# A two-layer transformer kernel on one core: idle products in the stops of layer 0, a tighter routing table, later last weights, and a tail with shared products first

## What is computed

```python
xn = _layernorm(x, axis=-1)
s = _L0_attn_ref(xn, w_qkv, w_out, ln_scale, ln_bias)   # 16 heads of 16, a = (q.k)**4, causal, a / sum(a)
g = _silu(_L0_ffn_ref(xn, ...))                         # 256 -> 2048 -> 256, 4-bit weights with scales
x = x + s * g
xn = _layernorm(x, axis=-1)
s = _L1_attn_ref(xn, Wq, Wk, Wv, Wo, bo)    # 16 heads of 128 in 4 groups, ALiBi, 30*tanh(s/30), causal softmax
g = _silu(_L1_ffn_ref(xn, ...))             # 32 experts, top 4 by sqrt(softplus(logits)) + bias, plus a shared one
x = x + s * g
```

## Time and profile before

| | |
|---|---|
| Time, median of 3 runs | 853.99 us (852.8 to 854.36) |
| The profiled execution: its own time | 852.75 us |
| The profiled execution: span of its trace | 850.9 us |
| Mean granted clock of PE | 0.98 |
| PE busy | 783.5 us (92%) |
| DVE busy | 609.0 us (72%) |
| ACT busy | 465.7 us (55%) |
| POOL busy | 422.4 us (50%) |

### The profile page before, as it was taken

One profiled execution on the slowest core, in us unless ns is written; L12 is line 12 of the kernel. 1 busy time (PEld: TensorE's weight loads), 2 busy tenths in 40 slices (PEclk: granted clock), 3 DMA queues, 4 the chain that ended last, 5 costly groups with the idle time before them and its releaser, 6 DMA issues.

```text
span 850.9 us, 13950 instructions
## 1 busy us (share of the span) xinstructions
PE 783.5 (92%) x4871; PEld 637.8 (75%) x4871; DVE 609.0 (72%) x1077; ACT 465.7 (55%) x822; POOL 422.4 (50%) x479
## 2 busy tenths in 40 slices
PE   7999999978788878899998999999999997989996
PEld 6776776754233257698998989989999997978884
DVE  7588868457999867878788877997777543445455
ACT  4433342278888733686855565556665724555431
POOL 1767827333555445456444534576656514555530
PEclk9999999997999899999999999999999999999999
DMA  5211194000000040000000000010101599444107
GB/s 183 75 38 37 38 304 126 1 1 1 1 1 2 1 127 27 25 7 25 7 19 7 27 7 7 26 44 32 39 32 46 210 244 382 132 124 112 46 11 237
DMA packets 50115, 59.81 MB, mean 70 GB/s; under 512 B 13559, under 2 KB 41084, under 8 KB 50048
## 3 DMA queue, kind: packets, MB, share of 16 engines
q1 hardware_dynamic: 45488, 50.49, 19.2%
q0 software_dynamic: 4560, 8.44, 2.8%
HBM read 41.11 MB, written 21.86 MB: 74 GB/s over the span
## 4 chain that ended last, share of the span: by engine, by line
PE 58%; DVE 8%; POOL 6%; ACT 6%; issue 4%; DMA 3%; POOLq 0%; ACTq 0%; DVEq 0%; SPq 0%
PE ps L786 12%; PE ps L516 9%; PE ps L518 8%; PE ps L517 8%; PE ps L879 4%; PE ps L876 3%; PE ps L910 3%; POOL A L1777 2%; DMA xa<-xg_scratch 2%; PE ps L613 2%; PE ps L698 2%; PE ps L558 2%; PE ps L858 1%; DVE cap L1477 1%; PE ps L795 1%
## 5 line engine op out<-in xcount | busy, mean ns | idle before, releaser
L786 PE MATMUL ps<-V,P 128*128 128x129 f32 x1152 | 150.7, 276 | 0.0
L1131 ACT ACTIVATE cap<-cap 128x1024 f32<-128x1024 f32 (+7 forms) x128 | 87.1, 680 | 110.3 <-DVE cap L1477 106.6
L786 PEld LDWEIGHTS ps<-V,P 128*128 128x128 f32 x1152 | 143.3, 192 | 2.7
L1477 DVE SCALAR_TENSOR_TENSOR cap<-dist,ps 128x1024 f32<-128x1024 f32 (+7 forms) x128 | 95.3, 750 | 28.7 <-PE ps L518 20.8
L1701 POOL TENSOR_SCALAR_AFFINE_SELECT P<-P 128x128 f32<-128x128 f32 x128 | 38.3, 299 | 143.7 <-ACT P L1136 143.3
L1833 POOL DMA_INDIRECT y_scratch<-y_sb,aux_s x63 | 62.1, 985 | 70.8 <-ACT y_sb L1176 40.3
L1136 ACT ACTIVATE P<-cap 128x1024 f32<-128x1024 f32 (+7 forms) x128 | 87.6, 685 | 4.1
L516 PE MATMUL ps<-q_hi,k_hi 128*128 128x512 f32 x192 | 71.8, 374 | 6.4 <-DVE cap L1477 5.0
L518 PE MATMUL ps<-q_lo,k_hi 128*128 128x512 f32 x192 | 67.0, 349 | 0.0
L517 PE MATMUL ps<-q_hi,k_lo 128*128 128x512 f32 x192 | 66.7, 347 | 0.0
L1629 DVE TENSOR_SCALAR gu<-ps 128x256 f32<-128x256 f32 (+1 forms) x63 | 28.9, 458 | 47.6 <-PE ps L876 16.8
(11 more groups left out here) (288 smaller groups left out, 2104.7 us busy)
## 6 DMA issues: line engine op xcount, KB each, us to landing
xg_scratch<-blank SPq DMA_DIRECT2D x1, 8127.0 KB, 31.1
xa<-xg_scratch SPq DMA_DIRECT2D x63, 128.0 KB
ew<-in_experts SPq DMA_DIRECT2D x3, 1920.0 KB, 12.3
y<-y_scratch SPq DMA_DIRECT2D x8, 512.0 KB, 5.8
pk<-in_packed SPq DMA_DIRECT2D x8, 384.0 KB, 3.1
pks<-in_scales SPq DMA_DIRECT2D x8, 384.0 KB, 4.1
ew<-in_experts SPq DMA_DIRECT2D x1, 3072.0 KB, 17.5
wqk<-in_wqk SPq DMA_DIRECT2D x20, 128.0 KB, 2.0
```

The source lines that it names most:

```text
L786: last = pe.matmul(ps[:, 4 + r % 2, o:o + D1 + 1], P1[:, h % 2, a:a + P], V1[:, j, h // REP, :], start=(j == 0), stop=(j == t))
L1131: act.activation(cap[:, n % 2, 0:w], cap[:, n % 2, 0:w], ACT.Tanh, scale=1.0 / (CAP * float(D1) ** 0.5))\
L1477: dve.scalar_tensor_tensor(out=cap[:, n % 2, 0:w], in0=dist[:, 0:w], scalar=slope, in1=psf[:, 1024 * (n % 2):1024 * (n % 2) + w], op0=ALU. ...
```

## The change

The change has five parts.

- **Early copies.** The copies of q and k of tiles 0 and 1 into `stack` move from behind the network of layer 0 into its steps 27 and 29 (ACT) and one step later (DVE). `turn_stack(0)` now stands ahead of PE's wait for `fT_ready`.
- **Idle products.** `keep_clock` gets new calls in layer 0's attention: one ahead of the scores of units 3 to 6, two ahead of each quad's turn (behind the wait for the banks, ahead of the wait for `o_raw`), two ahead of the last `turn_o`, one ahead of the projection. `add_nothing` adds products of the zero tile `blank` to bank 7 before the outputs of rows 4 and 5 of each quad.
- **Routing.** The two operations that follow the copy of the logits become a part of their own (number 37) at step 7. The four parts of the top 8 stand in one step each. Most later parts, the ranks and the sends stand about 8 steps earlier.
- **Last weights.** SP asks for the last group of experts behind the rows of block 15, where it was behind those of block 11.
- **Tail.** The loads of `y4` no longer wait for each other. The eight shared products stand ahead of all sums, each in a bank of its own, and `sum_rows` adds only the pairs. The pairs have four buffers. DVE multiplies by s one tile later, and POOL adds to x.

```diff
             for b in range(NT, NBLK):
                 sp.wait_ge(xg_ps, b - NT + 1)
                 load_rows(b)
-                if b == NT + 3:
+                if b == NT + 7:
                     load_experts(5)
...
             for t in range(NT):
-                if t >= YLOADS:
-                    sp.wait_ge(pair_ready, t - YLOADS + 1)
-                sp.dma_start(y4[:, t], y_dram.rearrange("(k t p) d -> t p k d", k=TOPK, p=P)[t]).then_inc(in_y4[t % YLOADS], 16)
+                sp.dma_start(y4[:, t], y_dram.rearrange("(k t p) d -> t p k d", k=TOPK, p=P)[t]).then_inc(in_xg[t], 16)
...
+            def add_nothing(n):
+
+                for _ in range(n):
+                    pe.matmul(ps[:, 7, 0:D], ident[:], blank[:, 0:D], start=False, stop=False)
...
+                if 3 <= n < 3 + LAG:
+                    pe.wait_ge(g0_ready, NT)
+                    keep_clock(1, 7)
                 bank_pair(("scores", n))
...
+                if half == 1 and j in (4, 5):
+                    add_nothing(2 if j == 4 or g == H0 // QUAD - 1 else 1)
                 pe.wait_ge(s0_four, BY_DVE0[DONE0[R] - 1])
...
             def turn_out0(g):
 
+                b = bank_pair(("turn", g))
+                keep_clock(2, b)
                 pe.wait_ge(o0_copied, g + 1)
-                b = bank_pair(("turn", g))
...
-            pe.wait_ge(fT_ready, 2 * NC)
             for t in range(NT):
                 turn_stack(t)
+                if t == 0:
+                    pe.wait_ge(fT_ready, 2 * NC)
                 turn_f0(t)
...
+            def shared_down(t):
+                if t == 0:
+                    pe.wait_ge(hT_copied, NBLK - NE)
+                    pe.wait_ge(y_copied, NBLK)
+                if t == 6:
+                    pe.wait_ge(s_added, NT * H1 // PAIR)
+                pe.matmul(sum_at(t), hs[:, t, 1, :], expert(NE)[:, 2, :], start=True, stop=False)
+
             def sum_rows(t):
                 pe.wait_ge(pair_ready, t + 1)
-                if t == 0:
-                    pe.wait_ge(y_copied, NBLK)
-                if t >= 2:
-                    pe.wait_ge(fth_ready, t - 1)
-                o = ps[:, 6 + t % 2, 0:D]
                 for i in range(2):
-                    pe.matmul(o, ident[:], yp[:, t % 2, i, :], start=(i == 0), stop=False)
-                pe.matmul(o, hs[:, t, 1, :], expert(NE)[:, 2, :], start=False, stop=True).then_inc(fin_ps, 1)
+                    last = pe.matmul(sum_at(t), ident[:], pairs_of(t)[:, i, :], start=False, stop=(i == 1))
+                last.then_inc(fin_ps, 1)
...
+                if s in STACK_STEPS:
+                    stack_hi(STACK_STEPS.index(s))
...
-                link(dve.tensor_copy(lg[:], o.rearrange("p (t e) -> p t e", t=NT)))
-                link(dve.tensor_scalar(r_a[:], lg[:], -1.0, None, ALU.mult))
-                dve.tensor_tensor(r_a[:], r_a[:], lg[:], ALU.max).then_inc(lg_read, 1)
+                dve.tensor_copy(lg[:], o.rearrange("p (t e) -> p t e", t=NT)).then_inc(lg_read, 1)
...
+                if s - 1 in STACK_STEPS:
+                    stack_lo(STACK_STEPS.index(s - 1))
...
-                dve.tensor_tensor(yp[:, t % 2], y4[:, t, 0:2], y4[:, t, 2:4], ALU.add).then_inc(pair_ready, 1)
...
+                if t >= 4:
+                    dve.wait_ge(fin_ps, t - 3)
+                dve.tensor_tensor(pairs_of(t), y4[:, t, 0:2], y4[:, t, 2:4], ALU.add).then_inc(pair_ready, 1)
...
+            for t in range(NT):
+                pool.wait_ge(mixed, NT + t + 1)
+                pool.tensor_tensor(x_tok[:, t, :], x_tok[:, t, :], mix1_b[:, t % 2, :], ALU.add).then_inc(x_ready, 1)
...
+STACK_STEPS = (2 * U0 - 5, 2 * U0 - 3)
+SUM_BANKS = (2, 3, 4, 5, 6, 7, 0, 1)
...
+          + [36, 37, 38, 39, 44, 44, 45, 46, 47]
...
-RANKS_AT = 7
+RANKS_AT = 6
```

More of the change, by code:

```diff
@@ L112 @@
 YRING = 6
-YLOADS = 4
 NO_ROW = 1 << 20
@@ L281, in build_program, with pairs_of @@
         y_sb = sb("y_sb", [P, YRING, D])
+        def pairs_of(t):
+            return yp[:, t % 2] if t % 4 < 2 else gu[:, t % 2].rearrange("p k m n -> p (k m n)").rearrange("p (i d) -> p i d", i=2)
         yp = sb("yp", [P, 2, 2, D])
@@ L367, in build_program @@
         in_aux = sem("in_aux")
-        in_y4 = [sem(f"in_y4{i}") for i in range(YLOADS)]
         y_sent = [sem(f"y_sent{i}") for i in range(YRING)]
@@ L567, in turn_f0, with keep_clock @@
                 last.then_inc(f_ps, 1)
+            def keep_clock(n, bank):
+                for _ in range(n):
+                    pe.matmul(ps[:, bank, 0:D], x_tok[:, 0, 0:P], x_tok[:, 0, :], start=True, stop=True)
+            def add_nothing(n):
+                for _ in range(n):
+                    pe.matmul(ps[:, 7, 0:D], ident[:], blank[:, 0:D], start=False, stop=False)
             def score_spans(n):
@@ L658, in gate_up @@
                 last.then_inc(done, 1)
-            def keep_clock(n, bank):
-                for _ in range(n):
-                    pe.matmul(ps[:, bank, 0:D], x_tok[:, 0, 0:P], x_tok[:, 0, :], start=True, stop=True)
             pe.wait_ge(in_x[0], 16)
@@ L971, in collect_f, with stack_hi @@
                     act.activation(fT[:, c, 0:HALF], ps[:, 4 + 2 * c, :], ACT.Copy).then_inc(fT_ready, 1)
+            def stack_hi(t):
+                act.wait_ge(qk_ready, t + 1)
+                if t >= 2:
+                    act.wait_ge(stk_ps, 4 * (t - 1))
+                for m, places in ((0, slice(0, 4, 2)), (1, slice(0, 2))):
+                    src = qk_tok[:, t, m * D:(m + 1) * D].rearrange("p (h a d) -> p h a d", h=H0, a=1)
+                    act.activation(stack[:, t % 2, m, :, places, :].bitcast(F32R),
+                                   src.to_broadcast((P, H0, 2, D0)), ACT.Copy).then_inc(stk_hi, 1)
             def high0(J):
@@ L1029, in _ @@
                     act.activation(hsd[:], hv[:], ACT.Sqrt).then_inc(sd_ready, 1)
+                if s in STACK_STEPS:
+                    stack_hi(STACK_STEPS.index(s))
             collect_f(2 * U0, dn0_ps, f0T)
             for t in range(NT + 1):
-                if t < NT:
-                    act.wait_ge(qk_ready, t + 1)
-                    if t >= 2:
-                        act.wait_ge(stk_ps, 4 * (t - 1))
-                    for m, places in ((0, slice(0, 4, 2)), (1, slice(0, 2))):
-                        src = qk_tok[:, t, m * D:(m + 1) * D].rearrange("p (h a d) -> p h a d", h=H0, a=1)
-                        act.activation(stack[:, t % 2, m, :, places, :].bitcast(F32R),
-                                       src.to_broadcast((P, H0, 2, D0)), ACT.Copy).then_inc(stk_hi, 1)
+                if 2 <= t < NT:
+                    stack_hi(t)
                 if t >= 1:
```

61 lines of the change are left out of this document (36 added, 25 removed).

## The result

The changed kernel takes 846.84 us (median of 6 runs, 846.22 to 847.45) where the kernel before took 852.67 us in the same comparison (median of 6 runs, 849.89 to 854.36). The ratio is 0.9926, with a 95% interval from 0.9905 to 0.9948. It is faster, by 5.8 us, and not by the 14.15 us of the prediction. 846.84 lies outside the range of 833.5 to 844.5. One execution of the experiments (of `last_quad_products_only`) took 1951.24 us and counts in no ratio.

The account below looks back on a forecast made before the run. PE was taken as the bound, busy 92% of the span, so gains come only from its idle or low-clock time. Gains 2.2 + 1.6 + 1.7 + 7.15 + 1.5 = 14.15 gave 838.6 to 839.8, middle 839.2 us, range 833.5 to 844.5.

Parts of the forecast that it names:

- Early copies, -2.2: Before layer 0's first scores: ACT sheds four copies, so 2.19 of PE's 2.58 us wait goes.
- Idle products, -3.0 + 1.4: Layer 0's attention: full clock gives back 3.0 us, products ahead of the turns cost 1.4, net gain 1.6.
- the cost of 1.4: Two idle products ahead of each turn cost 0.48 us in each of layer 0's inner three quads.
- The page's rule of half: Rival: PE sets the pace at low clock, so half the low time returns, 8.5 us instead of 3.0; 833.7 us, 7%.
- Routing, -1.7: Layer 1's attention: respaced routing parts shorten two PE waits that end with DVE, by 1.2 and 0.5 us.
- spread over four steps I take 1.2 of it: Layer 1: the top 8's four parts, one a step, take 1.2 us off PE's wait of 1.69 us.
- The last rival: Slower than before: newly placed routing makes PE wait at each part, 0.42 us each, 15.5 us in all; 856.4 us, 3%.
- Last weights, -7.15: Among the experts: asking for the last weights later removes the stall at block 12 and its low clock, 7.15 us.
- Tail, -1.5: End of the program: the rebuilt tail gains 1.5 us, taken between bounds of 0.2 and 3.7.
- With the 2.16 the end is 847.2: Tail without DVE and POOL holding each other: 2.16 us follow the last addition, end 847.2, a gain of 3.7.
- the serial tail: Rival: in the tail no DVE and POOL work overlaps, 1.85 us a tile, end about 850.7, gain 0.2; 840.5 us, 14%.
- all but the last two: The list of chances without its last entries, slower routing (3%) and something unseen (3%); the range was given 90%.

Follow-up runs that it names:

- last_quad_products_only: The changed kernel with layer 0's new idle products kept only at the end of the last quad; 850.91 us, ratio 0.9984.
- the first experiment: The changed kernel, but DVE adds to x again in the tail and POOL has nothing left to do there; 840.27 us, ratio 0.9855.

## Why the prediction was wrong, step by step

- **Early copies, -2.2:** right, 2.81 measured, 2.82 when undone. The whole wait of 2.58 us went, since PE's turn no longer waits for the copies of the sums either. Its row shows no wait at all.
- **Idle products, -3.0 + 1.4:** the direction was right, the size was not: 4.04 in the two spans, 5.0 when undone. The mis-sized term is the cost of 1.4. The two products at each turn do delay the first turn by 1 us, and a quad at full clock is not longer for it (23.33 against 23.32). The prediction says of the low clock that ACT sets the pace there; that the same slack takes in the products was not tested apart. Besides, the windows left out the end of the last quad, from 288.64 to 300.24, where the clock was 0.85. That quad alone gave 2.83 us where 1.22 was taken. The page's rule of half (the Trainium skill, "TensorE: Matmul & The Clock Gate", section "Terms") would have been worth 10.3 us here: the low time in the windows of the kernel before is 10.2 + 3.5 + 7.0 = 20.7 us. A fifth of that came back in the two spans, so the rule is far off in this stage. Whether it holds where PE sets the pace, no run here shows.
- **Routing, -1.7:** the wrong sign, +2.7. The step that failed is "spread over four steps I take 1.2 of it". The old wait did go, but the prediction looked only at what stood in front of the waits it knew, and not at what the new table puts in front of the next ones: the reciprocal of 1.75 us and two more parts of two operations each, in steps 30 and 31, ahead of the sums of the first output projection. With these three parts moved away 0.9 us came back. The other term, 0.5 for the wait of 1.98 us, came out. The last rival named the mechanism and priced it at every part, which was far too much. It needed a price at two or three places.
- **Last weights, -7.15:** the size came out (6.84), and the stall is gone from the place that was named, but the size is luck in good part. With both edits undone and the rest of the change kept, 4.9 of the 6.84 us stayed, and no run shows what gives them. The mechanism was half right too. By the prediction the moved load alone brings block 16 in time by 0.3 us (722.5 against 722.8). Alone it left a wait of 1.1 to 1.5 us there in four kernels. The tighter routing, with its earlier load of `aux_s`, takes the whole stall away by itself.
- **Tail, -1.5:** the wrong sign, +5.16, and the larger error. The step that failed is "With the 2.16 the end is 847.2". These 2.16 us had been read behind an addition on DVE, and were carried over to one on POOL. From the end of POOL's last instruction to the end of its closing it is 7.8 to 7.9 us in all five kernels that were read for it, and where POOL came last, the span ended 8.0 to 8.1 us behind it. The record was in the trace of the kernel before, at the line of the program's end, and no view that sorts by busy time or by waits shows it. Without it the new tail is worth what was forecast and more: 29.06 - 26.22 = 2.8 us with the additions on DVE, and 1.9 to 2.0 us in the three other kernels with that tail.
- **The shared ports** did what the earlier trace rows said, in small: a DVE operation of 0.69 us took 1.24 us beside POOL's 0.72 us. Had the two excluded each other all along, the last addition would have ended near 848.5 - 11.1 = 837.4 (the forecast serial end less what was gained ahead of the tail); it ended at 836.80. How the prediction got its 850.7 for the serial tail, from 1.85 us a tile against 1.76, is not in its working, so this agreement is worth little. The rule of the page "SBUF — State Buffer" (the Trainium skill, section "SBUF: two separate sides") agrees with the stretched rows. What it cost in all, with the handovers, is the 1.1 us of the first experiment.

Two of the sum's terms were turned round: the tail's by a record that stood in the trace of before, the routing's by what the new table put ahead of the sums. The other three (13.7 us) made nearly the whole forecast of 14.15, 4.9 us of them without a known cause. The prediction's 90% for its range is not the sum of its own list either: all but the last two add up to 94%.

## What to carry to other kernels

An engine that gets new work at the end of a program has to be looked up at the line of the program's end first: how long its closing takes, and when it began so far. In this kernel GpSimd's last instruction has to end about 8 us ahead of the end. When a table of placed parts is packed tighter, list for each new place what the slow engine waits for next on that queue, not only the waits that go away. Idle products ahead of a turn can cost nothing even if the trace shows that they delay it: here a quad at full clock took 23.3 us with them and without. And undo the parts of a change together as well as one by one: only that showed that most of the experts' gain had another source.

## What the runs showed of the hardware

- Closing of GpSimd: it ends 7.8 to 7.9 us behind its last instruction, whether that was a scatter to DRAM (9.5 us with what is left of it) or an addition in SBUF (8.6 us, of which 0.72 are the addition). The closings of PE, ACT and DVE took 0.4 to 1.6 us.
- The low clock comes and goes between kernels whose layer 0 is the same: two of the runs with all idle products had a spell at the first turn (the two products took 1.85 and 1.97 us instead of 1.13), and the stage took 117.2 instead of 115.5 us. The idle products do not rule low spells out, and their worth lies between 3.2 and 5.0 us accordingly (120.4 less 117.2 or 115.5).
